# Reordering one hand-over: the last attention chunk and the first expert of a fused attention and mixture-of-experts kernel

## The reference, cut to what matters

```python
mod = (_silu(c) @ wmod).reshape(2, 6, 1, -1)            # sa, ca, ga, sb, cb, gb
h = _layernorm(x) * (1 + ca) + sa
x = x + ga * attention(h, Wqkv, Wout)                   # 16 heads, keys i-127 .. i
h = _layernorm(x) * (1 + cb) + sb
probs = softmax(h @ gate_w.T + gate_b); top 2 of 8
for c in range(2):                                      # first, then second choice
    slot = expert * 640 + running count of that expert  # dropped from 640 on
    xbuf[slot] = h
    y += W2(relu(W1(xbuf) + b1)) + b2, gathered, times the probability
x = x + gb * y
```

## Time and profile before

| | us |
|---|---|
| median of 3 runs | 1161.39 |
| the profiled execution | 1163.25 |
| its span, first to last instruction | 1161.5 |
| TensorE busy in the span | 1096.3 (94%) |
| VectorE busy | 810.4 (70%) |
| ScalarE busy | 679.4 (58%) |
| GpSimd busy | 512.2 (44%) |
| mean granted TensorE clock | 0.99 |

### The profile page before, as it was taken

How to read it: one execution, slowest core, us unless ns; L and a number is a source line. 1 busy time by engine, 2 the same in 40 slices (tenths; PEclk the granted TensorE clock), 3 DMA queues, 4 the chain that set the end, 5 groups by cost and what they waited for, 6 DMA issues and landing times.

```text
span 1161.5 us, 25513 instructions
## 1 busy us (share of the span) xinstructions
PE 1096.3 (94%) x9548; PEld 719.8 (62%) x9548; DVE 810.4 (70%) x1735; ACT 679.4 (58%) x1892; POOL 512.2 (44%) x555
## 2 busy tenths in 40 slices
PE   7999999999999999999998897789999999999996
PEld 4455655655655655655656566455867768585865
DVE  6776586586587586586575777677877778687753
ACT  5676476476477476476475763537374654637361
POOL 2242264364265265265245565334344352524342
PEclk9999999999999999999999999889999999999998
DMA  9743000000000001000300015444345272634000
GB/s 333 142 166 112 19 1 24 33 2 29 29 1 29 29 1 37 20 2 32 92 1 33 19 41 124 103 116 72 98 97 141 57 163 75 156 105 82 23 19 9
DMA packets 109715, 77.46 MB, mean 67 GB/s; under 512 B 72842, under 2 KB 100634, under 8 KB 109340
## 3 DMA queue, kind: packets, MB, share of 16 engines
q1 hardware_dynamic: 98844, 54.32, 19.1%
q0 software_dynamic: 10752, 21.54, 6.2%
HBM read 49.99 MB, written 33.78 MB: 72 GB/s over the span
## 4 chain that ended last, share of the span: by engine, by line
PE 77%; issue 6%; POOL 6%; ACT 5%; DVE 5%; DMA 0%; SPq 0%; ACTq 0%; DVEq 0%; POOLq 0%
PE up L1579 18%; PE down L1594 17%; PE gen L560 11%; PE gen L651 6%; PE gen L574 6%; PE score L597 5%; PE pv L628 5%; PE pt L608 4%; PE pv L635 3%; ACT prob L860 2%; POOL probT_split L1353 1%; POOL probT_split L1355 1%; POOL h L366 1%; PE gen L659 1%; ACT probT L868 1%
## 5 line engine op out<-in xcount | busy, mean ns | idle before, releaser
L1620 ACT ACTIVATE hid<-up,b1T 128x512 f16<-128x512 f32 (+1 forms) x192 | 120.6, 628 | 187.7 <-PE up L1579 175.4
L1579 PE MATMUL up<-xT,w 128*128 128x512 f16 (+1 forms) x1152 | 214.7, 348 | 12.0 <-DVE xT L1488 10.4
L1353 POOL TENSOR_SCALAR_AFFINE_SELECT probT_split<-probT 128x512 f32<-128x512 f32 x128 | 101.4, 793 | 260.8 <-ACT probT L868 256.7
L1594 PE MATMUL down<-w,hid 128*128 128x256 f16 x1920 | 213.1, 273 | 1.1 <-issue 0.8
L1594 PEld LDWEIGHTS down<-w,hid 128*128 128x128 f16 x1920 | 187.5, 98 | 25.9 <-issue 1.3
L560 PE MATMUL gen<-hT,big 128*128 128x512 f16 x768 | 185.5, 381 | 7.4 <-ACT h2T L894 4.3
L860 ACT ACTIVATE prob<-score,negmax 128x128 f32<-128x128 f32 x512 | 180.7, 373 | 0.7 <-DVE negmax L1043 0.7
L1579 PEld LDWEIGHTS up<-xT,w 128*128 128x128 f16 x1152 | 113.2, 99 | 108.2 <-DVE xT L1488 10.7
L1681 POOL DMA_INDIRECT out<-y,tail x80 | 87.5, 1094 | 196.6 <-DVE y L1666 183.7
L1636 DVE TENSOR_TENSOR hid<-hid 128x512 f16<-128x512 f32 (+1 forms) x192 | 113.5, 604 | 78.3 <-ACT hid L1621 53.3
L868 ACT ACTIVATE probT<-pt 128x512 f32<-128x512 f32 x128 | 76.8, 600 | 95.8 <-PE pt L608 94.7
(11 more groups left out here) (156 smaller groups left out, 1544.6 us busy)
## 6 DMA issues: line engine op xcount, KB each, us to landing
slot_inputs<-empty_row SPq DMA_DIRECT2D x80, 129.5 KB, 2.6
raw<-slot_inputs SPq DMA_DIRECT2D x28, 320.0 KB
big<-in_L_ffn_W SPq DMA_DIRECT2D x28, 256.0 KB
big<-in_L_ffn_W SPq DMA_DIRECT2D x7, 1024.0 KB
out<-x SPq DMA_DIRECT2D x7, 512.0 KB
x<-in_L_attn_x SPq DMA_DIRECT2D x1, 3072.0 KB, 23.5
kept<-out,tail POOLq DMA_INDIRECT x80
out<-y,tail POOLq DMA_INDIRECT x80
```

Source lines behind the costliest of these rows:

```text
L1353: pool.affine_select(out=probT_split[:, h % 2, :, 1], in_=probT[:, h % 2], pattern=[[0, TILES], [1, P]], compare_op=ALU.is_ge, fill=zero, ...
L1579: mm = pe.matmul(bank, w1[:, par, kd, a, ft * P:(ft + 1) * P], part_rows(e, n, xT[:, par, b * KD + kd, :]), start=(i == 0), stop=(i == 5))
L1594: mm = pe.matmul(down[n][:, s, :], hid[:, ft, a, t * P:(t + 1) * P], w2[:, par, ft, b, :], start=(i == 0), stop=(i == 3 * FT - 1))
L1620: act.activation(part_rows(e, n, hid[:, ft, 0, :]), bank, ACT.Relu, scale=1 / W_SCALE, bias=bias).then_inc(hid_hi, 1)
```

## The change

It has seven parts. (1) EARLY_AT: each part of the early half's routing one step sooner. The early half's softmax now stands in VectorE's step 18 and its top 2 in step 19, ahead of that step's line 1179; both stood behind the loop. (2) SEND_AT: the eight sends of the chunk before, two in each of steps 13 to 16, become three, three and two in steps 13, 14 and 15. (3) LATE_OUT: the late half's output products no longer wait for the loop's end in a bank of the general pool; they accumulate in the second half of score bank 0, for heads' pairs 0 and 1 in step 16, 2 and 3 in step 17, 4 in step 18, and 5 to 7 behind the loop. The first up product into that bank waits for a new semaphore, late_free. (4) Part 0 is turned ahead of round NC's slots. (5) The late half's modulation comes after hidden_low 5 and not after 7. (6) Part 1 is turned ahead of the late half's softmax, and its counts come after the third of eight up blocks and not after the first. (7) Part 2 is turned ahead of the split of the next weights and of the second finish; it was between the second and third finish. Besides, the loads of a part go out choice by choice with a semaphore each, so the turn of a first choice can start before the second has landed.

```diff
-            EARLY_AT = {"add": 14, "stats": 15, "rstd": 16, "modulate": 16, "pack": 17, "low": 17, "turn": 18, "logits": 19}
+            EARLY_AT = {"add": 13, "stats": 14, "rstd": 15, "modulate": 15, "pack": 16, "low": 16, "turn": 17, "logits": 18}
+            LATE_OUT = {16: (0, 1), 17: (2, 3), 18: (4,)}
+            SEND_AT = {13: (0, 1, 2), 14: (3, 4, 5), 15: (6, 7)}
...
+            late_out = score[0][:].rearrange("p t n -> p (t n)")[:, 512:1024]
...
+                    def project_out_late(pairs):
+                        for j in pairs:
+                            pe.wait_ge(attn_lo, PAIRS * LAST + PAIRS + j + 1)
+                            for t in (2, 3):
+                                for n, (a, b) in enumerate(SPLIT_PRODUCTS):
+                                    mm = pe.matmul(late_out[:, (t - 2) * D:(t - 1) * D], ...
...
+                            if last and i in LATE_OUT:
+                                pe.wait_ge(exp_done, H * NC - 1)
+                                project_out_late(LATE_OUT[i])
...
-                        project_out_tile(late, 2, range(PAIRS - 1))
...
+                        project_out_late((5, 6))
                         route_counts(NC)
-                        project_out_tile(late, 3, range(3, PAIRS)).then_inc(late_full, 1)
+                        project_out_late((7,)).then_inc(late_full, 1)
...
                         for ft in range(FT):
+                            if ft == 1:
+                                pe.wait_ge(late_free, 1)
                             up_product(pe, 0, 0, 0, ft)
...
                             up_product(pe, 0, 0, 1, ft)
-                            if ft == 0:
+                            if ft == 2:
                                 route_counts(NC + 1)
...  VectorE, in the steps
+                            if last and i == EARLY_AT["logits"] + 1:
+                                route_top(NC)
                             if last:
                                 attn_low_part(c, i - 4)
+                            if last and i == EARLY_AT["logits"]:
+                                route_softmax(NC)
...  VectorE, behind the loop
-                        route_softmax(NC)
-                        route_top(NC)
                         lift_base(NC)
...
+                        turn_first_part(dve, 0)
                         route_slots(NC)
-                        turn_first_part(dve, 0)
-                        add_attention(c, 1)
+                        add_late_attention(c)
...
                             hidden_low(dve, 0, k_)
-                        part_modulate(NC + 1)
+                            if k_ == 5:
+                                part_modulate(NC + 1)
...
+                        turn_first_part(dve, 1)
                         route_softmax(NC + 1)
                         route_top(NC + 1)
                         lift_base(NC + 1)
-                        turn_first_part(dve, 1)
                         route_slots(NC + 1)
...
                         finish(dve, 0, 0, 0)
+                        turn_first_part(dve, 2)
                         for i in range(4):
                             split_low(dve, 1, 1, i)
                         first_batches(dve, 1)
-                        finish(dve, 0, 0, 1)
-                        turn_first_part(dve, 2)
-                        finish(dve, 0, 0, 2)
+                        for g in range(1, 3):
+                            finish(dve, 0, 0, g)
...  GpSimd, last chunk
-                            if last and at["send"] <= i < at["send"] + TILES:
-                                scatter(c, [i - at["send"]])
+                            if last and i in SEND_AT:
+                                scatter(c, SEND_AT[i])
...  loads of a part
-                for g in range(GROUPS):
-                    for m in range(K):
+                for m in range(K):
+                    for g in range(GROUPS):
                         sp.dma_start(raw[32 * g:32 * g + 32, 0, first_blocks(n, m)].bitcast(U16),
...
-                          .then_inc(raw_first[n], 16)
+                          .then_inc(raw_first[n][m], 16)
```

More of the change, by code:

```diff
@@ L310, in chunk_groups @@
                 if c == LAST:
[L311 removed]
+                    return names + [("counts_part", 0), ("h2T_part", 1), ("logits_part", 1), ("counts_part", 1)]
                 return names + projections_after(c) + out_groups
@@ L1454, in build @@
             raw_loaded = [sem(f"raw_loaded{i}") for i in range(2)]
-            raw_first = [sem(f"raw_first{n}") for n in range(len(NPART))]
+            raw_first = [[sem(f"raw_first{n}_{m}") for m in range(K)] for n in range(len(NPART))]
             rows_turned = sem("rows_turned")
```

51 lines of the change are left out of this document (30 added, 21 removed).

## The result

The changed kernel took 1157.85 us in the median of 11 runs (1152.47 to 1160.17), the kernel before 1163.0 on the same chip: ratio 0.9949, 95% interval 0.9937 to 0.9961, a gain of 5.9 us by the ratio (5.15 between the two medians) where 13.1 was forecast. Two later sets of 5 runs of the same program gave 0.992 (0.9908 to 0.9933) and 0.9919 (0.9899 to 0.9939), 9.3 and 9.4 us. The direction was right, and the size was never reached; the median lies outside the range of 1145.4 to 1154.5. The first interval doesn't touch the two later ones, though the program is the same: an interval tells the noise within one set of runs, and the three sets lie up to 0.3% apart. Ratios of different sets are compared with that in mind.

A forecast was written before the change was run, and what follows sets the result against it. TensorE bounds it: holes of 6.0 and 4.4 us ahead of up products, plus clock falls behind them (1.5 and 2.9). Expert 1 starts at 772.0 instead of 785.1, all terms -13.1: 1161.39 - 13.1 = 1148.3, range 1145.4 to 1154.5.

The forecast's parts named there:

- signs of being wrong: Marks named ahead: pv 15 after 707, round NC's slots after 713, any hole over 3 us, or POOL/DMA row ahead of finish 2.
- the clock's 1.5: Part 1's up products: with only 1.1 and 0.6 us of idle left ahead, the 1.5 us lost to the clock goes.
- group 2: Down groups 1 and 2, ahead of part 2: same small waits as before, 11.8 us, ending at 748.9.
- the 2.9 us of late products less 1.4 for late_free: Behind the loop: first up block starts 2.9 us sooner, at 711.05; the second's new wait eats 1.4, start 713.1.
- The order of turn 1: Ahead of part 1: up products start at 726.6 instead of 733.28, 6.7 us, most from the turn going first.
- No hole before part 2: Turn 2 ends at 746.2, TensorE needs it at 748.9: the hole (-4.4) and its clock loss (-2.9) go.
- Landing: Rows of part 1: first choice landed by 723.5, second at 725.2, turned at 726.4; 1.9 us counted for landing.
- Group 3: Down group 3 waits for hidden 23 behind VectorE's queue: end 766.8 instead of 764.5, +2.2 us.
- A: Rival, half the gain: walk 2 to 4 us too kind, long idle and clock fall return; gain 8.6, 1152.8; chance 0.18.
- B: Rival, the wait moves: finish 2 waits 3 us more for group 0's rows; gain 10.1, 1151.3; chance 0.08.
- C: Rival, slower: VectorE waits for part 2's rows with splits and finishes queued; at landing 762, 1165; chance 0.05.
- D: Rival, no effect: loop longer by 3.5, early turn brings nothing, part 1 lands late; gain under 2.3, 1160; chance 0.04.

The follow-up runs named there:

- r5_after_again: The changed kernel, unedited, run again in a later set: ratio 0.992 to the kernel before, profiled execution 1151.96 us.
- e1_split_first: The changed kernel with part 2 turned behind the four splits of the next weights, not ahead of them: ratio 0.9922 to the kernel before.
- r10: The kernel before with parts 5, 6 and 7 of the change alone (the orders of expert 0): ratio 0.9959 to the kernel before.
- r13_after_third: The changed kernel, unedited, once more in another set: ratio 0.9919 to the kernel before, profiled execution 1156.32 us.
- r16: The changed kernel with 36 unread products, in step 15 and around the late half's gate products: ratio 0.9906 to the kernel before.
- e4_old_turn1: The changed kernel with part 1 turned behind softmax, top 2 and lift, counts behind the first up block, as before: ratio 0.9967 to the kernel before.
- r8: The changed kernel with the early half's routing and the sends at their old steps: ratio 0.9953 to the kernel before.
- r9_before_warm: The kernel before with 50 and 38 unread products in the holes ahead of parts 1 and 2: ratio 0.9954 to the kernel before.
- r6_order: The changed kernel with VectorE's order finish 0, two splits, turn 2, finish 1, two splits, hidden 16, finish 2, the rest: ratio 0.9908 to the kernel before.

## Why the prediction was wrong

The milestones against my chain, as increments of lateness (each: measured less forecast, less the same of the milestone before). First profile after: pv 15 +1.6, part 1 +0.7, its ups' end (741.09, forecast 737.1) +1.7, part 2 +2.0, groups 3 and 4 with part 2's ups +1.5; sum 7.56 = 779.56 - 772.0. r5_after_again: -0.4, +1.1, 0, -0.9, +1.9; sum 1.6. Two of the signs of being wrong came in the first profile: pv 15 after 707 (707.18) and round NC's slots after 713 (713.53).

**The step that failed**: "The idle left is 1.1 and 0.6 us, both of a length that brought no fall, so the clock's 1.5 goes too", and with it the unspoken one that the loop keeps its clock. I had taken one 1.6 us hole that brought no fall for a rule. The idle in front of pv 12 is 2.43 to 2.66 us in the ten unfilled profiles with the new steps (1.54 to 1.64 in the four with the old ones: the new steps add 1 us, which I had put down to the sends before unit 13's mask and priced only as a wait; no run moves the sends alone); the clock fell behind it in three of them and stayed in seven. In front of part 1, the 18 ups took 5.63 after 0.80 of idle (e1_split_first) and 4.06 after 1.40 (r5_after_again). No length of idle in this range decides it. In the first profile the falls cost 1.3 in step 16, 1.7 in part 1 and 1.7 in group 3 (each: its row against the same row of r5_after_again): 4.7 of the 7.6. The other executions of that set look alike: nine of eleven have a mean clock of 0.990 to 0.994 (the profiled one 0.993), where all five of r5_after_again, with one fall in the profile, have 0.995. The Trainium skill says, on the page "TensorE: Matmul & The Clock Gate", Part 1, that the activity measure runs free of the program, so the same kernel meets it differently from run to run; the three unedited profiles agree: one fell at three places, two only in part 0.

**The second term: group 2.** I gave groups 1 and 2 11.8 us from the earlier trace rows. From the first down product to part 2's first up product it is 10.9 in r5_after_again and 13.85 in the first profile after; in six of the eighteen profiles (after, r10 and r13 to r16) it is 13.8 to 16.8, in the rest, less the wait for a turned part or what fills it, 10.9 to 11.8. In the six TensorE does a few products at a time, mostly one to three, with 0.3 to 1.1 us between, and waits for nothing that the profile shows. I had no such term. Little of it reaches expert 1, since groups 3 and 4 would wait for VectorE anyway: from group 1 to expert 1 the four stalled profiles r13 to r16 take 36.3 to 37.8 us and the first profile 36.8 without its fall in group 3 (38.47 - 1.67), against 35.9 to 36.1 without a stall. In the first profile that is 0.9 of the 7.6. What stalls it stays open. None of the eight profiles of the sets e1 to e4 and r5 to r8 has it, and all four of r13 to r16 have it, so it may go with the set or its chip. The DMA engines are at 0.5 to 0.9 there, and an instruction packet arrives in these microseconds, but both hold for the profiles without a stall too. (The Trainium skill, "Runtime: NRT & Kernel Launch", section "Instruction fetch mechanics", has instructions fetched by DMA in blocks, mostly hidden; no run here shows that this fetch is what is late.)

With that, the 5.9 us between the first profile and r5_after_again are accounted for: 0.5 at the mark, 4.7 of falls and 0.9 of the stall make 6.1.

**The terms that held.** Late products and the steps: pv 15 at 705.16 in r5_after_again (forecast 705.6), and the 2.9 us of late products less 1.4 for late_free: part 0 at 710.37, its second block at 712.35 (711.05, 713.1). The order of turn 1: part 1 at 727.24 (726.6), shown by e4_old_turn1. No hole before part 2, and 10.52 for its 48, in the three unedited profiles. The clock's price: r9_before_warm.

**Landing.** I counted 1.9 us and got rows turned at 726.4; VectorE stood 2.5 to 2.6 us for the first choice and turned the second at 725.94 to 727.19 even in r5_after_again. That is the +0.7 to +1.1 at part 1. At part 2 turn 2 ended at 748.3 and not at 746.2; 1.0 of that is the later issue of the loads (740.33 for 739.3), the rest their landing.

**Group 3.** The wait for line 1666 came as forecast, but the term was mis-sized: +2.2 expected; with the 2.1 us late turn behind it, hidden 16 came at 759.08 and not at 757.0, and groups 3 and 4 took until 773.64, 14.5 from part 2's last up product (759.12) against 12.7: +1.8. e1_split_first and r6_order change nothing but VectorE's order and take 2.5 and 3.3 us off the stretch from group 1 to expert 1, so it is VectorE's queue: turn 2, put ahead of the splits by the change itself, stood 2.2 us for its rows with that queue behind it.

**The base.** I took 13.1 off a median of 1161.39, though the sum was made on an execution of 1163.25. r5_after_again came within 1.6 us of the chain (773.64), and the ratio in its set is 9.3 us, since before is 1161.6 there. So some of what the change removes wasn't in the faster executions of before, or the profiled one was late for another reason: 0.5 us of it stands at the mark (661.11 against 660.59). Of the rest no trace here shows where it lies. A slip besides: 785.1 is the end of the last down row; expert 1's start is 784.92, so the chain itself forecast 12.9.

Of the rivals, A was nearest in the first set (8.6 with one clock term lost), though by another way: the links of the chain held within about 1 us up to part 2 in r5_after_again, no idle of over 3 us came back, and in the first set's profile the clock fell all the same. B's mark, finish 2 behind a late DMA, isn't there; C and D are refuted by every profile.

## What to carry to other kernels

Where all that follows a point is one unbroken stretch, take the start of that stretch as the only number: here time = expert 1's start + 378.3 in 15 of 18 profiles (378.5, 379.1 and 379.4 in the others), and every gain is read there. Don't credit a clock term to a hole that is only shortened; give it as a range between kept and fallen, unless the idle is filled or gone, and take several executions of the kernel before as the base. When an engine's wait is removed, walk its queue on to the next consumer: turn 1's move won 7.4 us at part 2, of which 4.7 reached expert 1, and turn 2's place ahead of the splits cost 2.5, because low halves queued behind its wait. Before two executions are compared, line them up at a row ahead of the change: 3.7 of the 4.4 us of r13_after_third lay there.

## What was unexpected in the hardware

The same program, with 2.57 or 2.58 us of idle ahead of the same products, ran them at 1.2 GHz in one execution and at 2.4 in another (12 products in 2.76 and 1.47). Idle filled with unread products kept the clock in ten places of ten (r9_before_warm's two with them), where the two places of short idle, unfilled, saw 8 falls in 21. And TensorE can stand for 2.3 to 3.2 us in pieces in the middle of a group of 48 products, for nothing that the profile shows, in some executions and not in others; in two of six such cases the clock fell in the stall too, in all 5 to 6 us more for the two groups than without (15.9 and 16.8 against 10.9), though under 2 us of it reached expert 1. And the same program came 3.2 us later through its first 27 us in one execution than in another.
